# A third pair of PSUM banks for the gate and up products of a mixture-of-adapters feed-forward stage

## The reference

```
gate_base, up_base = xf @ Wg.T, xf @ Wu.T              # 512 -> 1408 each
base_out = silu(gate_base) * up_base @ Wd.T            # 1408 -> 512
for each adapter e (weight w_e, zero but for the top 2 of the router):
    h   = silu(gate_base + 2 xf Ag_e.T Bg_e.T) * (up_base + 2 xf Au_e.T Bu_e.T)
    acc = acc + w_e * 2 h Ad_e.T Bd_e.T
out = base_out + acc
```

## Time and profile before

| | us |
|---|---|
| median of 3 runs | 1650.46 |
| lowest and highest | 1649.22, 1653.79 |
| the profiled execution's own time | 1649.75 |
| its span in the profile | 1647.9 |
| PE busy in the span | 1406.0 (85%) |
| DVE busy | 1218.4 (74%) |
| ACT busy | 604.9 (37%) |

### The profile page before, as it was taken

The page is one execution under the profiler, slowest core; times in us unless marked ns, Lnnn a source line. Parts: engine busy times, 40 slices in busy tenths (PEclk is TensorE's granted clock), DMA queues, the critical chain, the costliest instruction groups (busy, mean ns, idle before and its releaser), DMA issues.

```text
span 1647.9 us, 16148 instructions
## 1 busy us (share of the span) xinstructions
PE 1406.0 (85%) x5768; PEld 685.0 (42%) x5768; DVE 1218.4 (74%) x1411; ACT 604.9 (37%) x1436; POOL 111.9 (7%) x116
## 2 busy tenths in 40 slices
PE   5756767999888799899889699899879788799999
PEld 2333433443333354444334255444334345454434
DVE  4899996589989766759998865759998967623330
ACT  5165553323223584232232376242333267211110
POOL 0000001001100000000110000100210000100000
PEclk8855558999999699899999779899999869789999
DMA  4167761123666631112656822012556741101112
GB/s 185 39 147 153 154 141 27 44 66 108 143 141 166 166 66 26 39 50 78 159 128 159 196 68 52 26 37 84 124 131 152 173 135 27 26 13 64 48 32 83
DMA packets 53278, 158.81 MB, mean 96 GB/s; under 512 B 5072, under 2 KB 10704, under 8 KB 44752
## 3 DMA queue, kind: packets, MB, share of 16 engines
q0 software_dynamic: 9216, 67.11, 19.8%
q1 hardware_dynamic: 25664, 54.23, 9.9%
q10 hardware_dynamic: 18320, 36.45, 8.6%
HBM read 86.20 MB, written 4.46 MB: 55 GB/s over the span
## 4 chain that ended last, share of the span: by engine, by line
DVE 30%; issue 30%; PE 29%; DMA 6%; ACT 4%; POOL 2%; DVEq 0%; ACTq 0%; POOLq 0%
DVE state L1091 11%; DMA y_sb<-state 5%; PE ps_a L894 5%; DVE state L1086 4%; PE ps_a L974 4%; PE ps_a L820 3%; DVE state L1096 3%; PE ps_b L834 3%; PE ps_w L873 3%; PE ps_a L906 3%; POOL rstd L477 2%; PE ps_b L914 2%; PE ps_w L782 2%; ACT r L625 2%; DVE neg_max L1126 2%
## 5 line engine op out<-in xcount | busy, mean ns | idle before, releaser
L894 PE MATMUL ps_a<-xt,w_sb 128*128 128x512 f32 x704 | 319.2, 607 | 0.0
L1091 DVE TENSOR_TENSOR_SCAN state<-decay,state 128x2048 f32<-128x2048 f32 x64 | 282.8, 4418 | 5.3 <-ACT decay L583 0.5
L677 ACT ACTIVATE r<-ps_a 128x512 f32<-128x512 f32 x132 | 78.6, 596 | 380.6 <-PE ps_a L906 202.8
L894 PEld LDWEIGHTS ps_a<-xt,w_sb 128*128 128x128 f32 x704 | 138.1, 197 | 174.9 <-issue 174.9
L820 PE MATMUL ps_a<-r 32*128 32x512 f32 (+3 forms) x512 | 140.4, 634 | 81.7 <-ACT r L625 55.2
L906 PE MATMUL ps_a<-r,wb_sb 128*128 128x512 f32 x352 | 177.1, 628 | 35.9 <-DVE r L1267 33.7
L583 ACT ACTIVATE decay<-dt_sb,decay_rate 128x511 f32<-128x511 f32 x256 | 162.9, 712 | 104.9 <-DVE state L1096 72.2
L1260 DVE SCALAR_TENSOR_TENSOR r<-r,ps_a 128x512 f32<-128x512 f32 x132 | 89.9, 681 | 146.3 <-ACT r L677 146.3
L625 ACT ACTIVATE r<-ps_a,neg_max 128x128 f32<-128x128 f32 (+3 forms) x256 | 133.6, 534 | 116.6 <-DVE neg_max L1126 116.1
L974 PE MATMUL ps_a<-wd_sb,r 128*128 128x512 f32 x352 | 162.4, 613 | 0.0
L1086 DVE TENSOR_TENSOR state<-du_sb,bc_sb 128x2048 f32<-128x2048 f32 x64 | 146.3, 2286 | 4.7 <-DMA y_sb<-state 4.6
(11 more groups left out here) (120 smaller groups left out, 1475.7 us busy)
## 6 DMA issues: line engine op xcount, KB each, us to landing
y_sb<-state POOLq DMA_DIRECT2D x64, 1024.0 KB, 9.7
bc_sb<-bc_rows ACTq DMA_DIRECT2D x64, 512.0 KB, 5.1
w_sb<-in_w_tiles SPq DMA_DIRECT2D x44, 512.0 KB, 3.7
wd_sb<-in_w_down SPq DMA_DIRECT2D x44, 256.0 KB, 3.5
wb_sb<-in_w_adapt SPq DMA_DIRECT2D x44, 128.0 KB, 2.1
xa<-in_x SPq DMA_DIRECT2D x4, 1024.0 KB, 5.2
out_x<-xb SPq DMA_DIRECT2D x16, 256.0 KB, 7.0
xn_att<-in_ctx_t SPq DMA_DIRECT2D x4, 512.0 KB, 6.1
```

Source lines behind the costliest of these rows:

```text
L894: mm = nc.tensor.matmul(ps_a[:, 2 * (f % 2) + half, :], w_sb[:, slot, at + k * P:at + (k + 1) * P], xt[:, k, :], start=(k == 0), stop=Fals ...
L1091: nc.vector.tensor_tensor_scan(flat, decay[:, n % 2, :, :].rearrange("p j l -> p (j l)"), flat, 0.0, ALU.mult, ALU.add).then_inc(scan_chai ...
```

## The change

Tile f's two products get one of three pairs of banks instead of two: `GU_PLACE` gives 0 or 1 for a pair of `ps_a` and 2 for the two banks of `ps_w`, which tiles 4 and 7 use. Base product f waits for the evaluation (g, 2) of the tile g that had the pair before it; tile 4, the first in `ps_w`, waits for the last users of its two banks instead. The order changes: base 4 comes behind add (2,2) and the down adapters that follow it, and from there on base f + 2 stands where base f + 1 stood (5 within tile 3, 6 within 4, up to 9 within 7). None is left for tile 8, and base 10 stands within tile 9 as before. `EVAL` follows: (2,2), (4,0), (3,1), (5,0), (3,2), (4,1), (6,0), (4,2) and so on up to (9,0), (7,2), (8,1), (8,2), (9,1). The scan's pieces keep to k = 1 and k = 2. Slots and loads of `w_sb` and `wb_sb` and SP's order stay as they are.

```diff
--- before.py
+++ after.py
@@ -57,9 +57,15 @@
 
 
 
+BEGUN_INSIDE = {0: 1, 1: 2, 2: 3, 3: 5, 4: 6, 5: 7, 6: 8, 7: 9, 9: 10}
+BEGUN_AFTER = {2: 4}
+GU_PLACE = [0, 1, 0, 1, 2, 0, 1, 2, 0, 1, 0]
+GU_BEFORE = [max([g for g in range(f) if GU_PLACE[g] == GU_PLACE[f]], default=None) for f in range(FT)]
 EVAL = [(0, 0)]
 for _f in range(FT):
-    EVAL += [(_f, 1)] + [(_f + 1, 0)] * (_f + 1 < FT) + [(_f, 2)]
+    EVAL += [(_f, 1)] + [(_g, 0) for _f2, _g in BEGUN_INSIDE.items() if _f2 == _f]
+    EVAL += [(_f, 2)] + [(_g, 0) for _f2, _g in BEGUN_AFTER.items() if _f2 == _f]
+assert sorted(EVAL) == [(f, k) for f in range(FT) for k in range(3)]
 EVAL_AT = {fk: e for e, fk in enumerate(EVAL)}
 EVALS = len(EVAL)
 STEPS = MT * NT * 2
@@ -369,6 +375,10 @@
             def end(self):
                 assert self.n == self.per, (self.semaphore, self.n, self.per)
 
+        def gu_bank(f, half):
+            place = GU_PLACE[f]
+            return ps_w[:, half, :] if place == 2 else ps_a[:, 2 * place + half, :]
+
         def use(name, b, ffn=False):
 
             if ffn and isinstance(b, int) and b == BATCH - 1:
@@ -674,7 +684,7 @@
                 act.wait_ge(gu_ready, t * EVALS + e + 1)
                 if e >= 2:
                     act.wait_ge(h_ready, t * EVALS + e - 1)
-                nc.scalar.activation(gate[:, e % 2, :], ps_a[:, 2 * (f % 2), :], ACT.Tanh, scale=0.5)\
+                nc.scalar.activation(gate[:, e % 2, :], gu_bank(f, 0), ACT.Tanh, scale=0.5)\
                     .then_inc(tanh_ready, 1)
 
 
@@ -887,11 +897,16 @@
                 slot = f % 2
                 of_slot = (FT - slot + 1) // 2
                 pe.wait_ge(w_loaded[slot], 16 * (t * of_slot + f // 2 + 1))
-                if f >= 2:
-                    pe.wait_ge(h_ready, t * EVALS + EVAL_AT[f - 2, 2] + 1)
+                if GU_BEFORE[f] is not None:
+                    pe.wait_ge(h_ready, t * EVALS + EVAL_AT[GU_BEFORE[f], 2] + 1)
+                elif GU_PLACE[f] == 2:
+                    last = [("lowg", 0), ("lowu", 0)] if t == BATCH - 1 else [("dt", JT - 2), ("dt", JT - 1)]
+                    for name in last:
+                        bank, count = use(name, t, True)
+                        pe.wait_ge(work_free[bank], count + 1)
                 for half, at in ((0, WG), (1, WU)):
                     for k in range(KT):
-                        mm = nc.tensor.matmul(ps_a[:, 2 * (f % 2) + half, :],
+                        mm = nc.tensor.matmul(gu_bank(f, half),
                                               w_sb[:, slot, at + k * P:at + (k + 1) * P], xt[:, k, :],
                                               start=(k == 0), stop=False, skip_group_check=True)
                 mm.then_inc(gu_ready, 1)
@@ -903,7 +918,7 @@
                     pe.wait_ge(wb_loaded[f % 2], 16 * (t * of_slot + f // 2 + 1))
                 pe.wait_ge(h_ready, t * EVALS + EVAL_AT[f, k - 1] + 1)
                 for half, at in ((0, BG), (1, BU)):
-                    mm = nc.tensor.matmul(ps_a[:, 2 * (f % 2) + half, :], wb_sb[:, f % 2, at:at + P],
+                    mm = nc.tensor.matmul(gu_bank(f, half), wb_sb[:, f % 2, at:at + P],
                                           low[:, 2 * half + k - 1, :], start=False, stop=(k == 2),
                                           skip_group_check=True)
                 mm.then_inc(gu_ready, 1)
@@ -955,15 +970,18 @@
                 for f in range(FT):
                     add_slot(t, f, 1)
                     beside(EVAL_AT[f, 1])
-                    if f + 1 < FT:
-                        base(t, f + 1)
-                        beside(EVAL_AT[f + 1, 0])
+                    if f in BEGUN_INSIDE:
+                        base(t, BEGUN_INSIDE[f])
+                        beside(EVAL_AT[BEGUN_INSIDE[f], 0])
                     if f == FT - 1:
                         down_adapters(t, f - 1)
                     add_slot(t, f, 2)
                     beside(EVAL_AT[f, 2])
                     if 0 < f < FT - 1:
                         down_adapters(t, f - 1)
+                    if f in BEGUN_AFTER:
+                        base(t, BEGUN_AFTER[f])
+                        beside(EVAL_AT[BEGUN_AFTER[f], 0])
                 if b is not None:
                     transpose_normed("att", "xt", b, False)
                 down_adapters(t, FT - 1)
@@ -1255,16 +1273,15 @@
             def evaluate(t, e):
 
                 f, k = EVAL[e]
-                bank = 2 * (f % 2)
                 dve.wait_ge(tanh_ready, t * EVALS + e + 1)
-                stt(gate[:, e % 2, :], gate[:, e % 2, :], 1.0, ps_a[:, bank, :], ALU.add, ALU.mult)\
+                stt(gate[:, e % 2, :], gate[:, e % 2, :], 1.0, gu_bank(f, 0), ALU.add, ALU.mult)\
                     .then_inc(gate_chain, 1)
                 if k > 0 and f >= 2:
 
                     dve.wait_ge(d_done, t * FT + f - 1)
                 dst = hb[:, f, :] if k == 0 else hk[:, (2 * f + k - 1) % 4, :]
                 dve.wait_ge(gate_chain, t * EVALS + e + 1)
-                tt(dst, gate[:, e % 2, :], ps_a[:, bank + 1, :], ALU.mult).then_inc(h_ready, 1)
+                tt(dst, gate[:, e % 2, :], gu_bank(f, 1), ALU.mult).then_inc(h_ready, 1)
 
             def weigh_down(t):
                 dve.wait_ge(d_done, t * FT + FT)
```

## The result

| | before | after |
|---|---|---|
| median | 1652.12 us | 1674.69 us |
| lowest and highest of 4 | 1649.22, 1653.96 | 1668.71, 1677.8 |
| profiled execution, span | 1649.75, 1647.9 | 1668.71, 1666.9 |

The ratio is 1.0134 [1.0099, 1.0169]: slower, by 22.6 us. Timed again beside the experiments (`e0_after`) it was 1.015 [1.0131, 1.0169]. The forecast was 1677.

What follows compares the result with a forecast made beforehand. PE was taken to bound the stage's first half and the last batch, DVE the scan half. The first three batches' 19.4 us and the last's 7.8 make 27.2, on 1649.75 giving 1677 us; range 1665 to 1687.

Steps and rivals of the forecast that it cites:

- What bounds the stage: Evaluation stage: PE bounds the first half and the whole last batch, DVE the scan half; no bank holds PE up.
- base(4) ahead of add(3,1): First half of the first three stages: one more base on PE makes add(3,1) to add(5,1) 6.86 us later.
- Weight wait: PE waits 0.9 us for w_sb at each of base(6) to base(9), as its load stands behind wb's.
- The later waits in the scan half: First three batches: further weight waits hide, as PE takes 12.02 + 0.9 us a tile and DVE 15.6.
- First three stages: Eval(5,1) comes 7.76 us later, and each stage ends 6.46 us later; 19.4 us over three batches.
- One early evaluation: Scan half of the first three stages: eval(6,0) is already done, which saves DVE 1.30 us a stage.
- What the prediction put at 0 and kept in its range: First three batches: a slow restart at tile 10 may show through, some 0.9 us a batch; taken as 0, 2.7 in range.
- Tile 8 in the last batch: No base or down adapters stand between add(8,1) and add(8,2), so PE loses 2.47 us; 4.2 with the slow restart.
- The slow restart behind it: Last batch, add(8,2): after the idle time PE runs four passes at a mostly lower clock, 1.71 us more.
- Last stage: Last batch, bound by PE: four weight waits, 3.6 us, and tile 8, 4.2 us, make it 7.8 us longer.
- given back: Rival, chance 0.08: the first three batches' delay vanishes in later idle time; only the last batch counts, 1657.6 us.
- filled: Rival, chance 0.06: a base moved out of the scan half fills PE's idle time there; 20.6 us faster, 1629.

Runs made afterwards that it cites:

- e1_banks: The changed kernel's third pair of banks (tiles 4 and 7) with the order of before, base(f+1) within tile f: 1650.65 us, ratio 1.0.
- e9_early_down: Kernel before with tile 10 alone in the third pair, down tiles 0 and 1 ahead of down_adapters(10), transposes behind it: 1625.01 us, 0.9837.
- e2_loads: Changed kernel with the load of w(f+1) ahead of the load of wb(f) in SP's queue: 1666.0 us, 1.0092.
- e8_early_pieces: `e2_loads` with three scan steps moved forward to behind evaluation (2,2), ahead of (4,0), and three less in the down product's stretch: 1653.34 us, 1.0014.

## Why the prediction was right

- **What bounds the stage**: right. `e1_banks` at 1.0 shows that the base products lacked no bank. The down product at the stage's end did lack two, which the prediction did not look at (`e9_early_down`).
- **base(4) ahead of add(3,1)**, predicted 6.86 us: measured 6.88.
- **Weight wait**, predicted 0.9 each at base(6) to (9): from start to start with the restart, base(6) was late by 375.98 - 373.04 - 1.72 = 1.22 and its group by 0.10 more, 1.32 in the first stage. In the last batch the four came to 3.87 (0.95, 1.13, 1.03, 0.76), predicted 3.6. Base(5) and base(10) did not wait. `e2_loads` shows that the place in SP's queue is the cause; its stages are together 5.0 and 8.5 us shorter than in the two profiles of the change, and the 6.6 expected lie between; the 10.4 of the medians is more than the stages show, and the rest was not traced. The later waits in the scan half, costed at nothing (0.62 at base(7), 0.98 at base(8), 1.79 at base(9) in the first stage), were hidden, as predicted: DVE waits for none of the evaluations (5,1) to (9,2) of the first three stages.
- **First three stages**: eval(5,1) came 73.46 us behind add(0,1), before 65.26: +8.20 = 6.88 + 1.32, predicted 7.76. One early evaluation gives back: predicted 1.30, measured 8.20 - 7.25 = 0.95. The stage grew by 7.25, 7.22, 6.40, predicted 6.46 each. What the prediction put at 0 and kept in its range was there: DVE waits 0.62 us ahead of evaluation (10,1) in the first stage and 0.97 in the second, behind an add that restarted slowly, and not in the third:

```profile
457.84 3.40 PE L921 MATMUL ps_a<-r,wb_sb 128*128 128x512 f32 x4 [3.17 <-DVE r L1284]
```

- **Tile 8 in the last batch**: the dependence cost 4.08 - 1.72 + 0.10 = 2.46, predicted 2.47. The slow restart behind it, 1.71, was absent in one profile and there (1.69) in the other. That step took one instance for a rule.
- **Last stage**, predicted +7.8: measured +4.98 and +6.77. In the first, 3.87 + 2.46 = 6.33; the profile of before had a slow first add that this one has not (3.18 us from start to start against 1.79), which makes 4.94.
- **The rivals "given back" and "filled"**: both wrong. The delay reached the end. PE's idle time in the scan half was not the bound: with one base moved out of it, that half, from evaluation (5,1) to (10,2), went from 81.90 to 80.96 us, and not down by 6.86.
- **The time of 1677**: 27.2 us were added to the one profiled execution of before, all of them sure to reach the end. The medians are 22.6 and 25.5 us apart. Two profiles of the same kernel differ by 9.2 us, so that the number comes as close as 2.3 and 0.6 us to the medians is in part luck.
- **The reason for the delay in the first three batches** was told as PE's. `e8_early_pieces` points to the other side of it: the 6.9 us matter because DVE, the bound of the next half, has nothing to do meanwhile. With pieces at hand 12.7 us came back without a change in PE's order. It is not shown that they came back only for that, as the same pieces were not moved in the kernel before.

The prediction's estimate of 3.2 us for a 512 KB load, from the Trainium skill (DMA: Bandwidth & Descriptors, section Anatomy of one DMA), stays below every landing of the `w_sb` loads: the shortest was 3.5 after and 3.3 in `e2_loads`, the median 3.8 and 3.7.

## What to carry to other kernels

A further buffer helps only where the producer is held by a buffer: look at what stands in its timeline ahead of the consumer's wait. In this kernel, going a product further ahead starved the consumer once (4.90 us of DVE), moved the product away from the load that was timed for it, and left a later tile without cover, so other work of the consumer and the loads must move with it. Free banks were worth more where the producer waited for the consumer with finished inputs at hand: here at the end of the stage, where two down tiles done early in each batch gave 27 us over the whole.

## What the runs showed of the hardware

The same idle time of PE is not always followed by the lower clock. Behind 2.20 us four passes took 3.64 us in the profile of before, and 1.98 after, at 1596.73; behind 2.97 us the first add of the last stage took 3.35 us before and 1.95 after:

```profile
1470.94 3.35 PE L906 MATMUL ps_a<-r,wb_sb 128*128 128x512 f32 x4 [2.97 <-DVE r L1267]
```
```profile
1486.64 1.95 PE L921 MATMUL ps_a<-r,wb_sb 128*128 128x512 f32 x4 [2.97 <-DVE r L1284]
```

The difference is 1.4 to 1.7 us for one such restart. The two profiled executions of the change took 1668.71 and 1677.87 us, and PE was busy for 1400.4 and 1407.1 us with the same 5768 instructions, so 6.7 of the 9.2 us go with time at the lower clock. What decides between them was not found.
